# Last stage of a Trainium2 kernel without its two-place rings: rows summed and normalised where they were read, eight places for the statistics, stores awaited once at the end

## What is computed

```python
x = layernorm(x + attention(x))   # Fourier-feature attention, 16 heads of 8
x = layernorm(x + ffn(x))         # 8 experts, each row goes to its best 2
def _layernorm(x, axis=-1, eps=1e-05):
    m = jnp.mean(x, axis=axis, keepdims=True)
    v = jnp.var(x, axis=axis, keepdims=True)
    return (x - m) / jnp.sqrt(v + eps)
```

## Time and profile before

| what | value |
|---|---|
| time, median of 3 runs | 565.49 us (565.1 to 566.16) |
| the profiled execution | 564.61 us |
| its span | 562.8 us |
| busy: PE, DVE, ACT, POOL | 85%, 76%, 73%, 75% of the span |
| the last stage: 16 reads and 8 stores | from 528.4 us to the end |
| TensorE's granted clock, mean | 0.936 of full speed |

### The profile page before, as it was taken

How to read it: one execution, slowest core, us unless ns; L and a number is a source line. 1 busy time by engine, 2 the same in 40 slices (tenths; PEclk the granted TensorE clock), 3 DMA queues, 4 the chain that set the end, 5 groups by cost and what they waited for, 6 DMA issues and landing times.

```text
span 562.8 us, 12567 instructions
## 1 busy us (share of the span) xinstructions
PE 480.8 (85%) x4206; PEld 304.8 (54%) x4206; DVE 426.0 (76%) x880; ACT 409.5 (73%) x538; POOL 421.8 (75%) x464
## 2 busy tenths in 40 slices
PE   4499889999999999999999899686999999999300
PEld 2343344444444444444444343566999999999300
DVE  5578988988989989989989978243777776777362
ACT  2297689798898898898797887304877777688044
POOL 2079969899899899899899868472777777777343
PEclk9699999999999999999999999955999999999755
DMA  6685304506405406316116232422222222221471
GB/s 70 177 228 162 105 1 142 132 11 174 104 29 140 120 29 156 100 41 182 43 57 159 55 114 82 145 76 63 68 72 73 69 69 77 68 77 40 132 264 75
DMA packets 43928, 56.02 MB, mean 100 GB/s; under 512 B 8807, under 2 KB 30937, under 8 KB 43865
## 3 DMA queue, kind: packets, MB, share of 16 engines
q1 hardware_dynamic: 38993, 45.84, 30.5%
q0 software_dynamic: 4352, 9.02, 5.0%
q10 hardware_dynamic: 520, 0.36, 0.2%
HBM read 37.20 MB, written 18.00 MB: 98 GB/s over the span
## 4 chain that ended last, share of the span: by engine, by line
POOL 47%; PE 29%; issue 8%; DMA 5%; DVE 5%; ACT 4%; SPq 0%; ACTq 0%; DVEq 0%; POOLq 0%
POOL feats L1209 16%; POOL routed_dram L1277 13%; PE ang L687 10%; PE misc L696 10%; POOL parts L304 4%; POOL qk_f L302 3%; POOL parts L306 3%; POOL hot L1256 2%; PE misc L507 1%; POOL rstd L1217 1%; PE ang L678 1%; ACT feats L854 1%; PE ang L487 1%; POOL slot_k L1269 1%; DMA out<-feats 1%
## 5 line engine op out<-in xcount | busy, mean ns | idle before, releaser
L925 DVE TENSOR_SCALAR turns<-ang 128x1024 f16<-128x1024 f32 x128 | 155.3, 1216 | 36.5 <-PE ang L478 24.8
L747 ACT ACTIVATE feats<-ang 128x1024 f32<-128x1024 f32 x128 | 131.7, 1029 | 58.6 <-PE ang L487 56.5
L1209 POOL TENSOR_TENSOR feats<-feats 128x1024 f32<-128x1024 f32 x56 | 110.5, 1982 | 38.0 <-ACT feats L748 37.9
L748 ACT ACTIVATE feats<-ang 128x1024 f32<-128x1024 f32 x128 | 131.5, 1028 | 0.0
L816 ACT ACTIVATE feats<-weights_mem 128x1156 f32 x72 | 83.7, 1164 | 32.8 <-DVE feats L1156 28.4
L933 DVE TENSOR_TENSOR feats<-feats 128x1024 f32<-128x1024 f32 x72 | 106.8, 1484 | 0.7 <-ACT feats L748 0.6
L1277 POOL DMA_INDIRECT routed_dram<-rows_s,slots x64 | 83.4, 1303 | 18.8 <-issue 18.3
L1305 POOL DMA_INDIRECT expert_dram<-feats x72 | 70.7, 982 | 24.9 <-DVE feats L1156 15.4
L487 PE MATMUL ang<-turns,negi 128*128 128x512 f16 x256 | 77.5, 384 | 5.6 <-DVE turns L925 4.9
L687 PE MATMUL ang<-feats 128*128 128x128 f32 x576 | 78.2, 280 | 2.0 <-DVE feats L1111 2.0
L696 PE MATMUL misc<-feats 128*128 128x128 f32 x576 | 77.0, 278 | 0.0
(11 more groups left out here) (151 smaller groups left out, 593.3 us busy)
## 6 DMA issues: line engine op xcount, KB each, us to landing
weights_mem<-parts_dram SPq DMA_DIRECT2D x192, 96.0 KB
parts_dram<-parts SPq DMA_DIRECT2D x16, 384.0 KB, 4.2
feats<-routed_dram SPq DMA_DIRECT2D x72, 65.5 KB, 1.9
feats<-expert_dram SPq DMA_DIRECT2D x16, 256.0 KB, 5.7
x_all<-attn_x SPq DMA_DIRECT2D x8, 256.0 KB, 5.3
weights_mem<-ffn_W SPq DMA_DIRECT2D x8, 256.0 KB, 3.2
out<-feats SPq DMA_DIRECT2D x8, 256.0 KB, 2.0
x_in<-attn_x SPq DMA_DIRECT2D x7, 256.0 KB, 3.5
```

Source lines behind the costliest of these rows:

```text
L747: act.activation(f[:, 0, :], a, ACT.Sin, scale=TWO_PI)
L748: act.activation(f[:, 1, :], a, ACT.Sin, scale=TWO_PI / 2).then_inc(s["sines"], 1)
L925: dve.tensor_scalar(turns[:, u % 2, :], ang[:, slot(ph, u), :], MAGIC, -MAGIC, ALU.add, ALU.add)\
L1209: pool.tensor_tensor(f, f, f, ALU.mult).then_inc(s["sq_p"], 1)
```

## The change

The sum of a sequence's two halves is written over the first half, `y_back[:, n, 0]`, and the normalised rows over the second, `y_back[:, n, 1]`, from where they are stored. `y_sum` and `y_fin` are gone; the tensors of statistics, factors and offsets have eight places in place of two. With no place used twice, VectorE's wait for `fin_ok` and ScalarE's wait for a landed store are dropped. The eight stores count on one semaphore, `stored`, for which SP waits once, at the end, in place of two semaphores. No instruction is added, left out or moved on any engine: the same operations of the same shapes stand in the same order, with fewer waits and other addresses. In the code of the changed kernel, the lines of this stage have lower numbers (the add is L1174 in place of L1187).

```diff
--- before.py
+++ after.py
@@ -196,12 +196,10 @@
         tab_row = take(N_TILES).bitcast(U32)
         tab_e = take(N_TILES).bitcast(U32)
         y_back = fflat[:, 0:BATCH * TOPK * LEN].rearrange("p (r k t d) -> p r k t d", r=BATCH, k=TOPK, t=LT)
-        y_sum = take(2 * LEN).rearrange("p (r t d) -> p r t d", r=2, t=LT)
-        stats_f = take(2 * LT * 6).rearrange("p (r t n) -> p r t n", r=2, t=LT)
-        mv_f = take(2 * LT * 2).rearrange("p (r t n) -> p r t n", r=2, t=LT)
-        rstd_f = take(2 * LT).rearrange("p (r t) -> p r t", r=2)
-        shift_f = take(2 * LT).rearrange("p (r t) -> p r t", r=2)
-        y_fin = take(2 * LEN).rearrange("p (r t d) -> p r t d", r=2, t=LT)
+        stats_f = take(BATCH * LT * 6).rearrange("p (r t n) -> p r t n", r=BATCH, t=LT)
+        mv_f = take(BATCH * LT * 2).rearrange("p (r t n) -> p r t n", r=BATCH, t=LT)
+        rstd_f = take(BATCH * LT).rearrange("p (r t) -> p r t", r=BATCH)
+        shift_f = take(BATCH * LT).rearrange("p (r t) -> p r t", r=BATCH)
 
         ang = ctx.enter_context(nc.psum_tensor("ang", [P, 3, UC], F32))
         misc = ctx.enter_context(nc.psum_tensor("misc", [P, 2, 512], F32))
@@ -233,7 +231,7 @@
 
             "xT_t", "xT_e", "h_t", "h_e", "y_t", "y_e", "w_ok", "xb_ok", "pick1", "pick2", "y_at_ok",
 
-            "sum2", "fin_stat", "fin_aggr", "fin_eps", "fin_rstd", "fin_shift",
+            "sum2", "fin_stat", "fin_aggr", "fin_eps", "fin_rstd", "fin_shift", "stored",
             "fin_ok",
 
             "held",
@@ -242,7 +240,6 @@
         w2_in = [sem(f"w2_in{part}") for part in range(2)]
         x_in_sem = [sem(f"x_tile_in{r}") for r in range(RING_X)]
         y_sem = [sem(f"y_sent{r}") for r in range(UNROLL)]
-        fin_sem = [sem(f"stored{r}") for r in range(2)]
         y_in_sem = [sem(f"y_in{r}") for r in range(BATCH)]
         block = ctx.enter_context(nc.Block())
 
@@ -413,9 +410,8 @@
                     sp.dma_start(y_back[:, n, k, :, :], back[n, k]).then_inc(y_in_sem[n], 16)
             for n in range(BATCH):
                 sp.wait_ge(s["fin_ok"], n + 1)
-                sp.dma_start(out_rows[n], y_fin[:, n % 2, :, :]).then_inc(fin_sem[n % 2], 16)
-            for r in range(2):
-                sp.wait_ge(fin_sem[r], 16 * BATCH // 2)
+                sp.dma_start(out_rows[n], y_back[:, n, 1, :, :]).then_inc(s["stored"], 16)
+            sp.wait_ge(s["stored"], 16 * BATCH)
 
 
         @block.tensor
@@ -846,13 +842,9 @@
 
             def final_norm(n):
                 act.wait_ge(s["fin_shift"], n + 1)
-                if n >= 2:
-
-                    act.wait_ge(fin_sem[n % 2], 16 * (n // 2))
-                r = n % 2
-                for t in range(LT):
-                    ins = act.activation(y_fin[:, r, t, :], y_sum[:, r, t, :], ACT.Identity,
-                                         bias=shift_f[:, r, t:t + 1], scale=rstd_f[:, r, t:t + 1])
+                for t in range(LT):
+                    ins = act.activation(y_back[:, n, 1, t, :], y_back[:, n, 0, t, :], ACT.Identity,
+                                         bias=shift_f[:, n, t:t + 1], scale=rstd_f[:, n, t:t + 1])
                 ins.then_inc(s["fin_ok"], 1)
 
             for n in range(BATCH):
@@ -1178,21 +1170,16 @@
 
 
             for n in range(BATCH):
-                r = n % 2
-
                 dve.wait_ge(y_in_sem[n], 32)
-                if n >= 2:
-
-                    dve.wait_ge(s["fin_ok"], n - 1)
-                dve.tensor_tensor(y_sum[:, r, :, :], y_back[:, n, 0, :, :], y_back[:, n, 1, :, :], ALU.add)\
+                dve.tensor_tensor(y_back[:, n, 0, :, :], y_back[:, n, 0, :, :], y_back[:, n, 1, :, :], ALU.add)\
                     .then_inc(s["sum2"], 1)
                 dve.wait_ge(s["sum2"], n + 1)
                 for t in range(LT):
-                    ins = dve.bn_stats(stats_f[:, r, t, :], y_sum[:, r, t, :])
+                    ins = dve.bn_stats(stats_f[:, n, t, :], y_back[:, n, 0, t, :])
                 ins.then_inc(s["fin_stat"], 1)
                 dve.wait_ge(s["fin_stat"], n + 1)
                 for t in range(LT):
-                    ins = dve.bn_aggr(mv_f[:, r, t, :], stats_f[:, r, t, :])
+                    ins = dve.bn_aggr(mv_f[:, n, t, :], stats_f[:, n, t, :])
                 ins.then_inc(s["fin_aggr"], 1)
 
 
@@ -1308,15 +1295,13 @@
             tile_steps(steps)
 
             def scale_and_shift(n):
-
-                r = n % 2
                 pool.wait_ge(s["fin_aggr"], n + 1)
-                pool.tensor_tensor(rstd_f[:, r, :], mv_f[:, r, :, 1], eps_t[:, :], ALU.add).then_inc(s["fin_eps"], 1)
-                pool.tensor_tensor(shift_f[:, r, :], zero_t[:, :], mv_f[:, r, :, 0], ALU.subtract)
+                pool.tensor_tensor(rstd_f[:, n, :], mv_f[:, n, :, 1], eps_t[:, :], ALU.add).then_inc(s["fin_eps"], 1)
+                pool.tensor_tensor(shift_f[:, n, :], zero_t[:, :], mv_f[:, n, :, 0], ALU.subtract)
                 pool.wait_ge(s["fin_eps"], n + 1)
-                pool.tensor_tensor(rstd_f[:, r, :], rstd_f[:, r, :], half_t[:, :], ALU.pow).then_inc(s["fin_rstd"], 1)
+                pool.tensor_tensor(rstd_f[:, n, :], rstd_f[:, n, :], half_t[:, :], ALU.pow).then_inc(s["fin_rstd"], 1)
                 pool.wait_ge(s["fin_rstd"], n + 1)
-                pool.tensor_tensor(shift_f[:, r, :], shift_f[:, r, :], rstd_f[:, r, :], ALU.mult)\
+                pool.tensor_tensor(shift_f[:, n, :], shift_f[:, n, :], rstd_f[:, n, :], ALU.mult)\
                     .then_inc(s["fin_shift"], 1)
 
             for n in range(BATCH):
```

## The result

The changed kernel took 558.08 us (median of 5 runs, 555.39 to 566.18), the kernel before beside it 566.16 us (5 runs). The ratio is 0.9848, with a 95% interval of 0.981 to 0.9887: faster, by 8.6 us (6.4 to 10.8) of the 565.49 of before. The forecast was 6.4 us less and 559.1 us. Sign and cause were right and the size too small: 565.49 x 0.9848 is 556.9 us, under the low end of 558.0. Two more comparisons of the same kernel gave 0.9866 (0.9831 to 0.9901) and 0.9859 (0.9827 to 0.9891).

A forecast was written before the change was run, and what follows sets the result against it. The last stage was taken to be bound by its ring loop, 2.9 us per sequence. Add 7 coming 6.89 us earlier, minus 0.5 us for add and GpSimd interference, gave 6.4 us less: 559.1 us, range 558.0 to 560.9.

The forecast's parts named there:

- step 4: Last stage: VectorE's adds and GpSimd's small operations hinder each other, costing 0.5 us, within 0 to 1.45 us.
- What bounds the kernel: Last stage: a loop through add, statistics, scale and shift, activation and free place takes 2.9 us per sequence; no engine does.
- Step 1: Last stage, where timelines part: add 2 starts at 536.37 in place of 537.13, its data already in.
- Step 2: Last stage from add 2 on: VectorE paces at 1.93 us per sequence, so add 7 starts 6.89 us earlier.
- Step 3: Tail from add 7 to the last activation's end: 5.3 us, unchanged; then the last store takes its 2.0 us.
- Rival (b): Last stage: GpSimd's power operation blocks adds, period 2.16 us; 5.4 us less, 560.1 us; chance 0.12.
- (a): Last stage: the reads pace it, sequence 2 landing only just before use; 5.6 us less, 559.9 us; chance 0.10.
- (c): Last stage: stores become the bound, running one after another at 2.0 us each; 3 us less, 562.5 us; chance 0.03.
- (d): Last stage: adds and GpSimd's whole group take turns, 3.51 us per sequence; slower, 566.5 us; chance 0.02.
- (e): Last stage: the change does nothing, since something unseen in the DMA holds both ends; chance 0.03.

## Why the prediction was right in kind and too small

6.4 us were forecast and 7.1 to 7.3 measured in the last stage. The step that failed is step 4, the 0.5 us set aside for adds and GpSimd getting in each other's way: they cost 0.15. Steps 1 and 2 were too small by another 0.4 to 0.5 us. With 7.2 us less the time would be 558.3 us, inside the range. That it came out at 556.9 no step and no trace accounts for, and the range had too little room for it.

**What bounds the kernel** (first part): right. The two waits were on the path and carried all of it; with both back the gain is nil.

**Step 1, add 2**: 7.99 us after the first read's issue was forecast (536.37 - 528.38), 7.67 to 7.80 measured. The step took add 1 as fixed at 6.06; its reads landed 0.2 to 0.35 us sooner in the new profiles. That they would not delay add 2 was right.

**Step 2, the pace**: VectorE, as forecast, but 1.896 us and not 1.93. The pair that the 1.93 was read from starts with an add out of an idle spell, of 0.69 us; in an unbroken sequence every add takes 0.66. Over five periods 0.17 us. Steps 1 and 2 together: add 7 came 7.25 to 7.4 us earlier, not 6.89.

**Step 3, the tail**: the sum was right, what stood behind it was not. The step took the last store as what ends the program. It is GpSimd's drain, 2.2 us behind the store's landing. That did no harm here only because GpSimd's last operation happened to move forward by as much as the last activation (from 28.17 to 20.98 us), but it made the expectation for ScalarE's wait wrong by 2.1 us, and it hid where the next 2.6 us were.

**Step 4, the adds and GpSimd**: this term failed. It was set to 0.5 us and measured 0.15: VectorE wins every time, and only GpSimd's last group starts late, at 556.57, 2.21 us after add 7, where 2.06 stood before and 2.38 was forecast for this case. I had let the slipped L1304 begin only behind add 7; in the trace it is over at 555.08, 0.06 us after that add, and the next operation has started at 555.03. Nor was it a tie for long. At the first meeting, add 3, L1304 started 0.01 us behind the add. The 1.25 us that GpSimd was given from an add's end to L1304 (L1319 of the kernel before) had been read from a group whose first operation was the stretched one. When the last one is stretched, a whole group of four follows, one step of 0.15 us more: from the end of add 3 (546.78 + 0.66) to the next L1304 at 548.84 it is 1.40 us, and VectorE is at its next add after 1.23. The 0.5 us stood in the middle between a case that came and one that did not; nothing on record had made the other one as likely.

The Trainium skill, "SBUF — State Buffer", section "Who interferes with whom", has whoever starts first shut the other out for its whole length. Where an add was first, the traces agree, for the power operation too (1.49 us in place of 1.0, "Both waits back"). Where the power operation was first, they do not: an add 0.10 us behind its start took 0.69 us. Rival (b) rested on that half of it and did not come.

Together, steps 1, 2 and 4 make up the 0.7 to 0.9 us between the forecast and the last stage. The first ratio's 8.6 us has 7.2 within its interval (6.4 to 10.8). The later ratios give 7.6 (5.6 to 9.6) and 8.0 (6.2 to 9.8). All three middles lie above 7.2, but the medians of the three comparisons differ by 8.1, 6.7 and 9.0 us, on both sides of it. With a scatter of 526 to 532 us and more in the stages ahead, whether there is anything beyond the last stage to explain stays open.

**The range** was the other fault. It allowed 0.6 us to either side for the spread of runs, read off three runs that lay 1.06 us apart. The 23 runs of the kernel before taken later lie between 562.06 and 568.04, 17 others between 562.43 and 570.53. Even its medians in the four comparisons reach from 564.3 to 566.16. The range should have allowed more than a microsecond to either side for this.

**The rivals**: (a) did not come, since no add after 1 was released by a read; (c) did not, the last store landed 2.0 us after its issue as before; (d) did not, the period was 1.9 and not 3.3 us; (e) did not, the last stage is 7.2 us shorter.

## What to carry to other kernels

Where a ring place is freed by an engine further down the chain, count the ring's loop (here 5.8 us for two sequences, 2.9 for one) against the slowest engine's own work (1.9 us for one). The difference, 1.0 us for each of the five periods from add 2 to add 7, was the larger part of the 7.3 us by which add 7 moved. Of the rest, 1.0 is the earlier add 2, and 1.3, by subtraction, the one stop behind the slow first store. Try each wait by itself: without VectorE's the last activation came 4.3 us sooner, without ScalarE's 1.7, and without both 7.2. Look at what ends the program as well as at what ends the work: an engine that drains for 6 us should have its last operation early, and taking three sequences' small operations off it, and the last normalisation off ScalarE, was worth 2.6 us. And before giving a range, take the spread from many runs: three that agree say little when the stages ahead scatter by several us.

## What the runs showed of the hardware

- GpSimd's drain at the end of the program took 6215 to 6217 ns where its last operation took 0.2 us and 6575 to 6578 ns where that took 0.56 us, in all twelve profiles. It began with that operation and was over 6.0 us after the operation's end, and no program ended sooner. VectorE's drain of 0.41 us began with its last four aggregations, which take 0.38 us themselves. What GpSimd does in that time no run shows.
- A GpSimd operation that reads on-chip memory, begun while an add of two on-chip inputs ran, was held until the add's end: the small ones took 0.55 to 0.71 us in place of 0.20, the power operation 1.49 us in place of 1.0 (twice, begun 0.15 and 0.12 us behind an add). A power operation already under way held nothing off: adds begun 0.10 and 0.38 us behind its start took 0.69 us like the others.
- Two adds on VectorE with no wait between them start 0.58 us apart, though each is shown with 0.66 to 0.69 us.
- The same stages, with the same code, took from 524 to 537 us in the profiles taken, the long one with a granted clock of 0.69 between 20 and 40 us and 0.66 between 350 and 400, in place of 0.84 and 0.73. The profile with every add twice had 0.70 and 0.73 there and came to the last stage at 530.6. No run sets the clock, so that it is the cause is not shown.
